# The first slots of a fused retention and gated-FFN block re-ordered: other product order, load order, PSUM banks and cast order

## The reference

```
q, k, v, g = x@Wq, x@Wk, x@Wv, x@Wg              # 256, 256, 512, 512 wide, 4 heads
q, k = rotary(q), rotary(k)
o  = chunked retention(q, k, v, gamma per head)  # causal, decayed, a state carried along
x1 = layernorm(x + (rmsnorm(o)*gn * silu(g)) @ Wo)
h  = silu(x1 @ Wgate.T / 127) * (x1 @ Wup.T / 127)   # int32 weights, 768 hidden
out = layernorm(x1 + h @ Wdown.T / 127)
```

## Time and profile before

| | |
|---|---|
| median of 3 runs | 461.13 us (460.79 to 462.12) |
| the profiled execution | 462.0 us, of which the span 460.3 us |
| PE busy | 443.6 us, 96% |
| DVE, ACT, POOL busy | 295.6, 266.1, 228.3 us |
| loads and stores | 18.45 MB, 40 GB/s over the span |

### The profile page before, as it was taken

How to read it: one execution, slowest core, us unless ns; L and a number is a source line. 1 busy time by engine, 2 the same in 40 slices (tenths; PEclk the granted TensorE clock), 3 DMA queues, 4 the chain that set the end, 5 groups by cost and what they waited for, 6 DMA issues and landing times.

```text
span 460.3 us, 10359 instructions
## 1 busy us (share of the span) xinstructions
PE 443.6 (96%) x3286; PEld 398.3 (87%) x3286; DVE 295.6 (64%) x784; ACT 266.1 (58%) x794; POOL 228.3 (50%) x382
## 2 busy tenths in 40 slices
PE   7898999999999999999999999999999999999894
PEld 3677888899998889998889999888999988899893
DVE  3568666766656676666677566576765567654854
ACT  4588766555665466555556556555666555565451
POOL 2544255645545465543566354454654436552563
PEclk9899999999999999999999999999999999999998
DMA  7820101001110100101010010101001010100001
GB/s 238 271 109 1 47 2 47 12 25 34 36 36 14 57 11 23 34 15 54 11 57 11 23 34 16 52 11 42 15 34 34 11 36 12 37 1 13 22 26 38
DMA packets 15932, 18.45 MB, mean 40 GB/s; under 512 B 1440, under 2 KB 13728, under 8 KB 15904
## 3 DMA queue, kind: packets, MB, share of 16 engines
q1 hardware_dynamic: 15904, 18.09, 12.5%
HBM read 13.89 MB, written 4.19 MB: 39 GB/s over the span
## 4 chain that ended last, share of the span: by engine, by line
PE 89%; DVE 3%; ACT 2%; POOL 2%; DMA 2%; issue 1%; SPq 1%; POOLq 0%; DVEq 0%; ACTq 0%
PE b_rows L360 47%; PE b_ffn L360 19%; PE b_head L438 6%; PE b_head L413 3%; PE b_head L410 3%; PE b_state L360 3%; PE b_turn L467 3%; PE b_turn L374 3%; PE b_turn L427 2%; DMA wf_int<-in_w_proj 2%; DVE z L1018 0%; POOL rms L1206 0%; DVE yT_lo L994 0%; DVE y L1006 0%; SPq L277 0%
## 5 line engine op out<-in xcount | busy, mean ns | idle before, releaser
L360 PE MATMUL b_ffn<-x1T_hi,wf_hi 128*128 128x256 f32 x384 | 94.4, 283 | 0.7 <-issue 0.7
L360 PE MATMUL b_ffn<-x1T_lo,wf_hi 128*128 128x256 f32 x384 | 93.5, 281 | 0.0
L1187 POOL TENSOR_TENSOR h_lo<-wf_int,h_hi 128x256 fp32r<-128x256 f32 x96 | 69.7, 738 | 44.9 <-ACT h_hi L754 44.7
L360 PE MATMUL b_rows<-wp_hi,xT_hi 128*128 128x512 f32 x192 | 82.7, 431 | 3.6 <-POOL wp_lo L1236 1.8
L360 PE MATMUL b_rows<-wp_hi,xT_lo 128*128 128x512 f32 x192 | 77.0, 401 | 0.0
L360 PE MATMUL b_rows<-wp_lo,xT_hi 128*128 128x512 f32 x192 | 76.9, 401 | 0.0
L1204 POOL TENSOR_TENSOR ms_eps<-ms,eps 128x4 f32<-128x4 f32 x32 | 6.4, 199 | 140.3 <-ACT sq L718 140.3
L360 PEld LDWEIGHTS b_ffn<-x1T_hi,wf_hi 128*128 128x128 f32 x384 | 72.2, 188 | 2.1 <-issue 0.9
L360 PEld LDWEIGHTS b_ffn<-x1T_lo,wf_hi 128*128 128x128 f32 x384 | 72.5, 189 | 1.4
L939 DVE TENSOR_TENSOR wf_int<-b_ffn,wf_int 128x256 f32<-128x256 f32 x96 | 38.2, 421 | 51.7 <-ACT wf_int L743 51.6
L743 ACT ACTIVATE wf_int<-b_ffn 128x256 f32<-128x256 f32 x96 | 33.9, 382 | 52.0 <-PE b_ffn L360 51.4
(11 more groups left out here) (85 smaller groups left out, 1075.9 us busy)
## 6 DMA issues: line engine op xcount, KB each, us to landing
xT_raw<-in_xT SPq DMA_DIRECT2D x16, 256.0 KB, 3.0
x_sb<-in_x SPq DMA_DIRECT2D x16, 256.0 KB, 2.7
out<-wf_int SPq DMA_DIRECT2D x32, 128.0 KB, 1.7
wf_int<-in_w_ffn SPq DMA_DIRECT2D x6, 384.0 KB, 7.6
wf_int<-in_w_proj SPq DMA_DIRECT2D x6, 256.0 KB, 4.9
rope_sb<-in_rope SPq DMA_DIRECT2D x4, 256.0 KB, 7.1
wo_raw<-in_w_o SPq DMA_DIRECT2D x1, 512.0 KB, 7.1
gn_sb<-in_gn SPq DMA_DIRECT2D x1, 0.5 KB, 6.7
```

Of the source, the lines that this page charges most:

```text
L360: mm = pe.matmul(dst, a, b, start=(i == 0 and j == 0 and not begun), stop=(i == n - 1 and j == len(passes) - 1 and not more), skip_group_c ...
L1187: pool.tensor_tensor(h_lo[:, ring, hb], h_full[:, u], h_hi[:, ring, hb].bitcast(F32), ALU.subtract).then_inc(h_split[j], 1)
```

## The change

It does seven things, all in slots 0 to 6.

1. In slot 0 a product of a weight's high part waits only for the cast (`wp_high`) and the low product comes last in each group of three, where all three waited for the low part before.
2. Both pieces of the gate weights are loaded ahead of the first rotary table, and DVE makes all six low parts ahead of its first rotary product; POOL's share and the two semaphores `wp_split_g` go.
3. Slot 0's g goes to `b_ffn[0]` in place of a row bank, with no wait for the rotary products. One more product of zeros (`FILL`) stands between v and g in slot 0.
4. Slot 1 projects q and k before it turns tile 0's q and k.
5. Up to slot 5 the Wo product goes to the bank of k=4. The next slot's q and k wait only for the copy of v, and its v waits for `z1_ready`.
6. In slots 2 and 3 ACT casts the turned y before a piece of FFN weights.
7. In slot 3 x1 is turned after the g projection, where it was turned before it.

```
             load_w_proj(0)
             load_w_proj(1)
+            load_w_proj(2)
             sp.dma_start(rope_sb[:, 0], rope[:, 0]).then_inc(rope_in[0], 16)
-            load_w_proj(2)
...
+                if is_slot(s, 1) and c == 1:
+                    pe.wait_ge(rot_parts, 1)
+                elif without_down(s - 1) and c == 0 and exists(s - 1):
+                    pe.wait_ge(v_copied, s)
+                elif without_down(s - 1) and c == 1 and exists(s - 3):
+                    pe.wait_ge(z1_ready, s - 2)
+                elif not is_slot(s, 0):
+                    wait_bank(s, c, row_stages)
+                dst = g_bank(s, t) if c == 2 else row_bank(t, c)
                 if is_slot(s, 0):
                     for k in range(KD):
-                        if c < 2:
-                            pe.wait_ge(wp_split, KD * c + k + 1)
-                        else:
-                            pe.wait_ge(wp_split_g[k], 1)
-                        mm = split_product(row_bank(t, c)[:], stat[k:k + 1], mov[k:k + 1], k > 0, k < KD - 1)
+                        pe.wait_ge(wp_high, KD * c + k + 1)
+                        pe.matmul(dst[:], stat[k][0], mov[k][0], start=k == 0, stop=False, skip_group_check=True)
+                        pe.matmul(dst[:], stat[k][1], mov[k][0], start=False, stop=False, skip_group_check=True)
+                        pe.wait_ge(wp_split, KD * c + k + 1)
+                        mm = pe.matmul(dst[:], stat[k][0], mov[k][1], start=False, stop=k == KD - 1,
+                                       skip_group_check=True)
...
             def first_half(s, q, t, wide):
-                turn_qk(s, q, t)
+                if not is_slot(s, 1):
+                    turn_qk(s, q, t)
                 project(s, q, t, 0, qk_done)
+                if is_slot(s, 1):
+                    turn_qk(s, q, t)
                 gate_up_block(s - 1, q, t - 1, 2, wide)
                 project(s, q, t, 1, v_done)
+                if is_slot(s, 0):
+                    warm(FILL)
                 recall_and_score(s, q, t)
-                turn_x1(s, q, t)
+                if not is_slot(s, X1T_LAG):
+                    turn_x1(s, q, t)
                 project(s, q, t, 2, g_done)
+                if is_slot(s, X1T_LAG):
+                    turn_x1(s, q, t)
...
                 gate_v(s, q, t)
+                split_y(s, q, t)
                 if is_slot(s, 2) or is_slot(s, 3):
                     split_ffn(2 if s == 2 else 5)
-                split_y(s, q, t)
...
-            for c in range(2):
+            for c in range(3):
                 for k in range(KD):
-                    split_w_proj(c, k, wp_split)
+                    split_w_proj(c, k)
```

New functions that it calls:

```
        def without_down(s):
            return isinstance(s, int) and s < DOWN_LAG

        def wo_bank(s, t):
            return row_bank(t, 4 if without_down(s) else 3)

        def g_bank(s, t):
            return b_ffn[0] if is_slot(s, 0) else row_bank(t, 2)

            def warm(n):
                for _ in range(n):
                    pe.matmul(b_ffn[1][:], ones[:], attn[:].rearrange("p a b -> p (a b)"), start=True, stop=True)
```

More of the change, by code:

```diff
@@ L50 @@
 X1T_LAG, DOWN_LAG = 3, 6
-WARM_UP = 2
+WARM_UP, FILL = 2, 1
 FFN_LAG = 4
@@ L183, in build_block @@
         wp_high, wp_split = sem("wp_high"), sem("wp_split")
-        wp_split_g = [sem(f"wp_split_g{k}") for k in range(KD)]
         wo_scaled, wo_high, wo_split = sem("wo_scaled"), sem("wo_high"), sem("wo_split")
@@ L288, in _ @@
             load_x(0, 0)
-            sp.wait_ge(wp_split, 2 * KD)
-            for k in range(KD):
-                sp.wait_ge(wp_split_g[k], 1)
+            sp.wait_ge(wp_split, 3 * KD)
             for c in range(NFP):
@@ L385, in project @@
                     pe.wait_ge(xT_split, s + 1)
-                wait_bank(s, c, row_stages)
+                if is_slot(s, 1) and c == 1:
[7 more added lines that the diff above has]
+                dst = g_bank(s, t) if c == 2 else row_bank(t, c)
                 if is_slot(s, 0):
                     for k in range(KD):
-                        if c < 2:
-                            pe.wait_ge(wp_split, KD * c + k + 1)
-                        else:
-                            pe.wait_ge(wp_split_g[k], 1)
-                        mm = split_product(row_bank(t, c)[:], stat[k:k + 1], mov[k:k + 1], k > 0, k < KD - 1)
+                        pe.wait_ge(wp_high, KD * c + k + 1)
[4 more added lines that the diff above has]
+                                       skip_group_check=True)
                 else:
-                    mm = split_product(row_bank(t, c)[:], stat, mov)
+                    mm = split_product(dst[:], stat, mov)
                 mm.then_inc(done, 1)
@@ L497, in attention_out @@
                         pe.wait_ge(wo_split, 1)
-                    wait_bank(s, 3, row_stages)
+                    wait_bank(s, 4 if without_down(s) else 3, row_stages)
                     stat = [(yT_hi[:, h * P:(h + 1) * P], yT_lo[:, h * P:(h + 1) * P]) for h in range(H)]
                     mov = [(wo_hi[:, h, :], wo_lo[:, h, :]) for h in range(H)]
-                    split_product(row_bank(t, 3)[:, 0:D], stat, mov).then_inc(wo_done, 1)
+                    split_product(wo_bank(s, t)[:, 0:D], stat, mov).then_inc(wo_done, 1)
             def down(s, q, t, wide, parts=(0, 1, 2)):
@@ L522, in sum_wide @@
                 pe.matmul(b_ffn[0][:, 0:NFP], ones[:], wide_rows[:], start=True, stop=True).then_inc(wide_summed, 1)
+            def warm(n):
+                for _ in range(n):
+                    pe.matmul(b_ffn[1][:], ones[:], attn[:].rearrange("p a b -> p (a b)"), start=True, stop=True)
             def first_half(s, q, t, wide):
-                turn_qk(s, q, t)
+                if not is_slot(s, 1):
+                    turn_qk(s, q, t)
                 project(s, q, t, 0, qk_done)
+                if is_slot(s, 1):
+                    turn_qk(s, q, t)
                 gate_up_block(s - 1, q, t - 1, 2, wide)
                 project(s, q, t, 1, v_done)
+                if is_slot(s, 0):
+                    warm(FILL)
                 recall_and_score(s, q, t)
-                turn_x1(s, q, t)
+                if not is_slot(s, X1T_LAG):
+                    turn_x1(s, q, t)
                 project(s, q, t, 2, g_done)
+                if is_slot(s, X1T_LAG):
+                    turn_x1(s, q, t)
                 if is_slot(s, 2):
@@ L614, in _ @@
             pe.wait_ge(filled, 1)
-            for _ in range(WARM_UP):
-                pe.matmul(b_ffn[1][:], ones[:], attn[:].rearrange("p a b -> p (a b)"), start=True, stop=True)
+            warm(WARM_UP)
             pe.wait_ge(consts, 1)
@@ L696, in gate_v @@
                         act.wait_ge(y_ready, s - 1)
-                    act.activation(g_sb[:, t % 2], row_bank(t, 2)[:], ACT.Silu).then_inc(g_gated, 1)
+                    act.activation(g_sb[:, t % 2], g_bank(s, t)[:], ACT.Silu).then_inc(g_gated, 1)
             def split_y(s, q, t):
@@ L854, in _, with split_w_proj @@
         def _(dve):
-            def split_w_proj(c, k, signal):
+            def split_w_proj(c, k):
                 dve.wait_ge(wp_high, KD * c + k + 1)
                 dve.tensor_tensor(wp_lo[:, c, k], wp_raw[:, c, k], wp_hi[:, c, k].bitcast(F32),
-                                  ALU.subtract).then_inc(signal, 1)
+                                  ALU.subtract).then_inc(wp_split, 1)
             def halves(ap):
@@ L1017, in residual_1 @@
                         dve.wait_ge(x1_ready, n)
-                    dve.tensor_tensor(z1[:], row_bank(t, 3)[:, 0:D], x_sb[:, tn, :], ALU.add).then_inc(z1_ready, 1)
+                    dve.tensor_tensor(z1[:], wo_bank(s, t)[:, 0:D], x_sb[:, tn, :], ALU.add).then_inc(z1_ready, 1)
                     dve.wait_ge(z1_ready, n + 1)
@@ L1063, in slot @@
                 rotate_sin(s, q, t)
-                if is_slot(s, 0):
-                    split_w_proj(2, 1, wp_split_g[1])
                 hidden(s - 1, t - 1, 2)
```

3 lines of the change are left out of this document (removed).

## The result

The changed kernel takes 458.81 us (median of 8 runs, 458.44 to 459.39), the kernel before 460.81 us in as many (460.46 to 463.38). The ratio of all runs is 0.9944 with a 95% interval of 0.9927 to 0.9961: faster by 0.56%, 1.8 to 3.4 us; the two medians alone give 0.9957, since the kernel before has more long executions. The forecast was 457.8 in a range of 456.7 to 459.8.

What follows compares the result with a forecast made beforehand. PE, busy 96% of the span, was taken as the bound, leaving its stalls and lower-clock time to win. Terms 2.1 + 0.6 + 0.7 − 0.1 = 3.3 us, set against the median 461.13, gave 457.8, range 456.7 to 459.8.

Steps and rivals of the forecast that it cites:

- The front, 2.1: Slots 0 and 1: slot 1's scores on PE come at 17.46 in place of 19.56, 2.1 us earlier.
- The bytes ahead of that transfer are the same, in another order: Slot 0, input of tile 2: its transfer lands no earlier, so ACT's copy of v still ends at 14.05.
- the term doesn't hang on that order: Front: even if exchanging the loads brings nothing, g ends near 13.5, the copy of v is last, and 2.1 us stays.
- The recall of slot 2 keeps that wait: Slot 2: the recall's 0.5 us wait for y stays, since retention, squares and norm follow each other as before.
- The residual waits, 0.7: Projections behind the Wo product: four waits for the residual, 0.7 us in total, go.
- Slot 2, 0.6: Slot 2, before Wo: casting y earlier removes all of PE's 0.6 us wait for the low part of y.
- Slot 3, −0.1: Slot 3: the 0.34 wait before x1's turn goes, but PE waits 1.15 before Wo; net loss 0.1 us.
- lower bound of −0.4: Slot 3: z1's layer norm ends no earlier, and mask and rotary sums push x1's low part back; 0.4 us lost.
- The base: Whole kernel: 3.3 us off the profiled 462.0 gives 458.7; set against the median 461.13 it gives 457.8.
- the clock's fall: Rival, slot 1: PE's clock falls again and slot 1 runs at half speed until 17.05; gain 1.8, time 459.4; chance 0.22.
- in the way: Rival, slot 0: at low clock the product of zeros takes 1.8 us, slot 1 starts 1.2 later; 462.6, chance 0.04.

## Why the prediction was right, and where it was not

Right was the frame: what PE waits for in the first slots carries to the end one for one, slot 1 starts on ACT's copy of v (0.61 idle where 1.1 was expected), from there to the scores it takes 3.38 us as forecast, the clock stays up, and slot 3 gives nothing. The direction and the range held. The size at the median is 2.0 to 2.6 us, not 3.3, and by the terms of the sum:

- **The front, 2.1.** Between the traces it was 2.77, as the input of tiles 2 and 3 landed 0.78 earlier than the sum assumed. "The bytes ahead of that transfer are the same, in another order" was true and the conclusion was wrong: in all ten traces with the weights issued one behind the other it landed earlier than in the four with a rotary table between them. The step "the term doesn't hang on that order" failed outright: undone by itself, the exchange costs 2.0 us, 1.4 of them through POOL's scaling of Wo meeting the rotary sums. The prediction had put those sums at 1.28 and hidden; with the old order they took 2.49 and were not.
- **"The recall of slot 2 keeps that wait."** This step failed: the wait grew by 1.0. The argument followed the chain from the retention to y and found each link moved by the same amount. It left out the list of DVE beside the chain, which slipped by 1.1 and locked POOL out at the moment at which the chain needed it (0.20 became 1.24).
- **The residual waits, 0.7.** Mechanism right, size off by two: 0.39, 0.38 and 0.42 in slots 3, 5 and 6 and 0.13 in slot 4, where ACT's copy of the turned q and k was next: 1.3, and 1.25 when undone.
- **Slot 2, 0.6.** 0.74 at its place, but worth 0.3 to 0.4 when undone, since slots 3 and 4 take most of it back.
- **Slot 3, −0.1.** It was −0.38. DVE's list was rightly named as the bound. The turn of x1 is worth nothing in either place. The prediction's lower bound of −0.4 had the result but for one link: it had the norm of z1 held up. That norm took 0.41 and x1 was ready by 35.63; the rotary sums took 1.84 beside v_lo and POOL's next instruction and pushed the low part of x1 back.
- **The base.** The gain worked out against one execution was set off from the median of the others in full. The sum took that execution's lower clock for a part of the kernel, and by the recorded clocks at least 16 of 81 executions of before, and likely over half, do without it. The 37 with the lowest clocks have a median of 462.05, 3.2 above the changed kernel, near the sum; the 16 have 460.6, 1.8 above it. So about 1.4 of the sum is not there in a usual execution, where the prediction took off 0.87 of time but nothing of the gain. This is read from medians and mean clocks; no execution without the fall was traced.

The terms of the traces, 2.77 − 1.02 + 0.74 + 0.39 − 0.38 + 0.13 − 0.03 + 0.38 + 0.42, give 3.4. That the forecast's sum was 3.3 is luck: a front and residual waits that gave 1.3 more than forecast hide a loss of 1.0 in slot 2.

Of the rivals, the clock's fall didn't come in the changed kernel's trace, nor after 1.40 us of idle time without the product of zeros, and the product of zeros was neither in the way nor of use.

On the lock, the Trainium skill ("SBUF — State Buffer", section "SBUF: two separate sides") says that of a DVE instruction with two SBUF inputs and a GpSimd instruction that reads SBUF, the one that starts first has the shared ports for its whole length and the other is fully blocked. The addition of the norm agrees with it: 1.24, 0.54, 0.42 and 0.20 as the subtraction ends later or earlier. The prediction quoted the rule, weighed it for the norm of z1, and didn't ask where else it applied. It also misread the order there: the rows have that norm start at 37.78, 0.03 ahead of v_lo, not while it ran, so the rule as worded would have let it through, and yet it took 1.46. For a start as close as this the rows and the rule differ, and why isn't shown.

## What to carry to other kernels

A term that is "hidden" or "moved with the rest" has to be checked on every engine that shares something with the chain, not on the chain alone; write down what runs on DVE and POOL at the same moment. When all of a front moves, it doesn't move rigidly: in one list the slip of 1 us made a tiny instruction six times as long. And compare traces over a stretch that leaves out what differs from one execution of the same kernel to the next. And undo each edit of a bundle by itself: here the exchange of two lines of loads was worth 2.0 us and the bank of the Wo product 1.2, slot 1's new order lost 0.7, and the product of zeros and the place of x1's turn did nothing. Three parts were never undone alone: the order of the products in slot 0, DVE's making of all six low parts, and the bank of slot 0's g.

## What was not expected of the hardware

- The issue of one transfer on SP's queue took 1.43 to 2.02 us in the four traces in which a rotary table was issued between the weights, and 0.56 to 0.72 in the ten in which it came behind them, with the same bytes issued ahead. Why isn't shown.
- A wait that the trace gives as 0.17 us of idle time behind four small products cost 0.4 us: in slots 3, 5 and 6 of the kernel before, and in slot 3 with the Wo product in its old bank.
- PE ran its products of slot 0 at full pace (0.23 us from start to start, where it didn't wait) from 7.18 on in the changed kernel's trace and from 7.31 on in the second trace of the kernel before, and at 0.43 until about 10 in the first, with a granted clock of 1.00 in the records of all three.
- The same kernel (the one before) ran with the lower clock at the front in some executions and without it in others: of 81 mean granted clocks 37 are at 0.989 to 0.993, as in the two traces with the lower stretch, and 16 at 0.998 or 0.999, which leaves no room for it.
- DVE's cast of Wo's high part, 0.68 us elsewhere, took 1.77 when it began 0.05 us after POOL's v_lo.
